# Routing the last quarter of the tokens of four mixtures of experts through sorted tiles

## The reference, cut to what matters

```
xn     = layernorm(x)
logits = xn @ gate_w + gate_b              # 16 experts (layers 0, 3) or 8 (layers 1, 2)
i0, i1 = the two largest logits            # gates g0, g1 = softmax over these two
layers 0, 3 (SwiGLU):  f_e(t) = (silu(t @ w1[e]) * (t @ w2[e])) @ w3[e]       # hidden 128
layers 1, 2 (GELU):    f_e(t) = gelu(t @ W1[e] + b1[e]) @ W2[e] + b2[e]       # hidden 256
x     += g0 * f_i0(xn) + g1 * f_i1(xn)
```

## Time and profile before

| | us |
|---|---|
| median of 3 runs | 1806.35 |
| lowest, highest | 1804.22, 1815.67 |
| span of the profiled execution | 1807.2 |
| TensorE matmuls busy | 1678.7 (93%) |
| VectorE busy | 1077.2 (60%) |
| ScalarE busy | 966.8 (53%) |
| GpSimd busy | 871.1 (48%) |

### The profile page before, as it was taken

How to read it: one execution, slowest core, us unless ns; L and a number is a source line. 1 busy time by engine, 2 the same in 40 slices (tenths; PEclk the granted TensorE clock), 3 DMA queues, 4 the chain that set the end, 5 groups by cost and what they waited for, 6 DMA issues and landing times. The chain is left out here.

```text
span 1807.2 us, 32921 instructions
## 1 busy us (share of the span) xinstructions
PE 1678.7 (93%) x12503; PEld 955.4 (53%) x12503; DVE 1077.2 (60%) x1532; ACT 966.8 (53%) x1427; POOL 871.1 (48%) x730
## 2 busy tenths in 40 slices
PE   5879999999689999998999997999999769999998
PEld 3635555554244444444444445777777535555554
DVE  6667777766863332365334236666656467777766
ACT  2545555555236666526666645666666355555554
POOL 3318887877025333313333335333323008877777
PEclk8999999999799999998999998999999879999999
DMA  5004343333202222401222340000000004333333
GB/s 126 1 15 118 108 111 111 110 109 101 74 1 79 90 83 66 103 2 32 93 79 67 96 95 1 1 2 1 2 1 1 3 5 122 116 118 116 114 116 103
DMA packets 74948, 121.64 MB, mean 67 GB/s; under 512 B 18306, under 2 KB 22594, under 8 KB 74146
## 3 DMA queue, kind: packets, MB, share of 16 engines
q1 hardware_dynamic: 74786, 119.48, 22.7%
HBM read 115.74 MB, written 3.67 MB: 66 GB/s over the span
## 5 line engine op out<-in xcount | busy, mean ns | idle before, releaser
L766 POOL TENSOR_TENSOR x<-x,mx_gated 128x512 f32<-128x512 f32 x254 | 326.7, 1286 | 85.6 <-DVE mx_gated L718 83.4
L711 DVE TENSOR_TENSOR mx_hidden<-ps,mx_hidden 128x1024 f32<-128x1024 f32 (+1 forms) x256 | 246.2, 962 | 177.2 <-PE ps L579 176.7
L579 PE MATMUL ps<-tokens_high,w_high 64*128 64x512 f32 x1536 | 330.9, 427 | 8.7 <-ACT mx_hidden L873 5.0
L873 ACT ACTIVATE mx_hidden<-ps,w_bias 128x1024 f32<-128x1024 f32 x256 | 264.1, 1115 | 124.8 <-PE ps L579 124.8
L579 PE MATMUL ps<-tokens_high,w_low 64*128 64x512 f32 x1536 | 305.7, 393 | 0.0
L579 PE MATMUL ps<-tokens_low,w_high 64*128 64x512 f32 x1536 | 305.5, 393 | 0.0
L919 POOL TENSOR_TENSOR x<-x,mx_gated 128x512 f32<-128x512 f32 x126 | 161.5, 1282 | 253.3 <-DVE mx_gated L891 253.3
L891 DVE SCALAR_TENSOR_TENSOR mx_gated<-ps,w_bias,mx_gates 128x512 f32<-128x512 f32 x128 | 96.0, 750 | 280.1 <-PE ps L843 260.6
L694 ACT ACTIVATE mx_hidden<-ps 128x1024 f32<-128x1024 f32 x256 | 248.5, 1022 | 15.4 <-PE ps L579 1.4
L1884 DVE TENSOR_TENSOR c_near_weights<-c_near_hats 128x768 f32<-128x768 f32 x192 | 190.0, 1037 | 102.8 <-PE ps L1755 102.8
L648 PE MATMUL ps<-mx_hidden,w_second 128*64 128x512 f32 x1024 | 248.4, 605 | 0.4 <-DVE mx_hidden L711 0.4
(11 more groups left out here) (225 smaller groups left out, 1905.6 us busy)
## 6 DMA issues: line engine op xcount, KB each, us to landing
mx_gates<-gate_board SPq DMA_DIRECT2D x768, 128.0 KB, 3.1
w_first<-in_f_first SPq DMA_DIRECT2D x4, 1024.0 KB, 11.6
c_weight<-in_c_weight SPq DMA_DIRECT2D x1, 2304.0 KB
x<-in_x SPq DMA_DIRECT2D x8, 256.0 KB, 5.8
w_second<-in_f_second SPq DMA_DIRECT2D x4, 512.0 KB, 13.3
w_first<-in_f_first SPq DMA_DIRECT2D x4, 512.0 KB, 9.8
out_x<-x SPq DMA_DIRECT2D x16, 128.0 KB, 2.7
gate_board<-xn SPq DMA_DIRECT2D x56, 16.0 KB, 2.1
```

Source lines behind the costliest of these rows:

```text
L579: last = pe.matmul(out[h], weights[w][half(h), w_own], tokens[t][half(h), t_own], start=(p == 0), stop=(p == 2))
L711: dve.tensor_tensor(own, second[:, 0:halves, :], own, ALU.mult).then_inc(s.hidden.semaphore, 1)
L766: pool.tensor_tensor(place, place, gated[:, n % GATED, :], ALU.add).then_inc(s.added.semaphore, 1)
L873: act.activation(hidden[:, n % HIDDEN, f], first[:, (n * F + f) % BLOCKS], ACT.Gelu, bias=w.bias1[:, e * F + f:e * F + f + 1]).then_inc(s. ...
```

## The change

Of each layer's 8 chunks, 6 stay dense. The tokens of the last two (2048 tokens, 4096 pairs of token and expert) are sorted by expert:

1. TensorE transposes the normed tokens (lay: 8 transposes) and ScalarE copies them.
2. The choice of the last pair of chunks is made first, and 24 small VectorE operations and two matmuls against a triangle of ones (op, count_up) give each pair its slot. Each expert starts a new tile of 256 slots, so there are 32 tiles in a SwiGLU layer (16 + 16 experts) and 24 in a GELU layer.
3. GpSimd writes the tokens to a DRAM board with 32 indirect DMAs of 128 rows of 256 bytes (scatter). SyncE loads the board back (load, 3 or 4 DMAs of 512 KB) and fetches each tile's expert weights through a register (fetch: two register reads and four DMAs for a turn, a ring of 6 turns).
4. All engines leave the dense loop at one point (step 60 of 96, or 30 of 48) for a phase of 16 (GELU: 12) turns of two tiles, in plain float32. For each turn TensorE makes 2 transposes, 4 matmuls of 256 columns, 2 (GELU: 4) output matmuls of 256 columns and 2 transposes back. ScalarE copies the columns, activates and copies the output. VectorE multiplies (SwiGLU) and copies the turned tile.
5. SyncE stores the result to a second board, GpSimd gathers it with 32 indirect DMAs, VectorE weighs it (2 operations per unit, 2 units), TensorE transposes and sums it (merge: 16 matmuls in all), and VectorE adds it to x (by.add).
6. While GpSimd issues indirect DMAs, VectorE makes the adds of the dense steps (by_vector): steps 30 to 53 and 60 to 83 of a SwiGLU layer, steps 15 to 25 and 31 to 41 of a GELU layer.
7. The sorted board is filled with zeros once, during conv0 (4 DMAs of 512 KB). The banks of PSUM 6 and 7 are handed out by a list (OutBanks), and semaphores of conv0 are used again.

```diff
+        self.dense = CHUNKS - 2 * sorted_pairs
+        self.sorted_tiles = sorted_pairs * 2 * HALVES * CHUNK // P
+        self.tiles = self.sorted_tiles + experts
+        self.slots = 2 * self.tiles
+SWIGLU = Mixture(experts=16, hidden=128, sorted_pairs=1)
+GELU = Mixture(experts=8, hidden=256, sorted_pairs=1)
...
+class ByExpert:
+    TILE = 2 * P
+    RING = 6
+    GROUP = 16
+    def scatter(self, pool, i):
+        choice, t = i % 2, i // 2
+        if i == 0:
+            pool.wait_ge(self.k.cleared, self.k.cleared_all)
+            self.s.rows.wait(pool, 1)
+            self.s.laid.wait(pool, self.UNITS)
+        pool.indirect_dma_start(out=self.sorted_board, in_=self.laid[:, t // HALVES, half(t % HALVES)], in_offset=None,
+                                out_offset=bass.IndirectOffsetOnAxis(ap=self.rows[:, choice, t:t + 1], axis=0)).then_inc(
+                                    self.s.scattered.semaphore, 16)
+    def gather(self, pool, i):
+        unit, choice, t = i // 16, i % 2, i // 2
+        if i == 0:
+            self.s.stored.wait(pool, 16 * (self.m.slots // self.GROUP))
...
+    def fetch(self, sp, u):
+        if u == 0:
+            self.s.expert.wait(sp, 1)
+        if u >= self.RING:
+            self.s.out.wait(sp, u - self.RING + 1)
+        for a in range(2):
+            tile = a * self.TURNS + u
+            e = sp.value_load(self.expert[0:1, tile:tile + 1], min_val=0, max_val=self.E - 1)
+            landed = self.s.weights[u % self.RING].semaphore
+            sp.dma_start(self.first[half(a), u % self.RING, :],
+                         self.first_of[bass.ds(e, 1)].rearrange("e c n -> (e c) n")).then_inc(landed, 16)
+            sp.dma_start(self.second[:, u % self.RING, a, :],
+                         self.second_of[bass.ds(e, 1)].rearrange("e c n -> (e c) n")).then_inc(landed, 16)
+    def load(self, sp):
+        self.s.scattered.wait(sp, 16 * 2 * self.NT)
+        for g in range(self.m.slots // self.GROUP):
+            sp.dma_start(self.own_group(g), self.group(self.sorted_board, g)).then_inc(self.s.loaded[g].semaphore, 16)
+    def phase_tensor(self, pe):
...
+        columns(0)
+        for u in range(TURNS):
+            if u + 1 < TURNS:
+                columns(u + 1)
+            first_layer(u)
+            if u >= 1:
+                second_layer(u - 1)
+            if u >= 2:
+                turn_back(u - 2)
...
...
+    TURN_AT, AFTER = 9, 60
+    LAY_AT, COUNT_AT, MERGE_AT = (4, 6), 19, (77, 87)
+    SCATTER_AT, GATHER_AT, EACH = 32, AFTER + 2, 3
+    by = ByExpert(k, ctx, m, name, layer, top_two, hidden[:].rearrange("p r h c -> p (r h c)"), fetch_at=(38, 40, 42, 44, 46, 48), load_at=54, after=AFTER)
+    def by_vector(n):
+        return SCATTER_AT - 2 <= n < SCATTER_AT + ROUNDS or GATHER_AT - 2 <= n < GATHER_AT + ROUNDS or n == STEPS - 1
...
+        def gate_both(n):
+            gate(n)
+            gate(n + 1)
+            for a in (n, n + 1):
+                if by_vector(a):
+                    gates.add(dve, a, gated[:, a % GATED, :])
...
+            for a in (n - 3, n - 2):
+                if a >= 0 and not by_vector(a):
+                    gates.add(pool, a, gated[:, a % GATED, :])
+            for i in range(EACH):
+                if 0 <= (n - SCATTER_AT) // 2 * EACH + i < MOVES:
+                    by.scatter(pool, (n - SCATTER_AT) // 2 * EACH + i)
+                if 0 <= (n - GATHER_AT) // 2 * EACH + i < MOVES:
+                    by.gather(pool, (n - GATHER_AT) // 2 * EACH + i)
...
+    TURN_AT, AFTER = 3, 30
+    LAY_AT, COUNT_AT, MERGE_AT = (4, 6), 9, (39, 44)
+    SCATTER_AT, GATHER_AT, EACH = 15, AFTER + 1, 3
+    by = ByExpert(k, ctx, m, name, layer, top_two, hidden[:].rearrange("p r f h c -> p (r f h c)"), fetch_at=(16, 18, 20, 22, 23, 24), load_at=26, after=AFTER)
```

More of the change, by code:

```diff
@@ new lines, with __init__, bank, free @@
+class OutBanks:
+    def __init__(self, k, order, by_expert):
+        self.k, self.order, self.by_expert = k, order, by_expert
+        self.at = {use: i for i, use in enumerate(order)}
+    def bank(self, *use):
+        return self.k.ps[:, 6 + self.at[use] % 2, :]
+    def free(self, pe, *use):
+        i = self.at[use] - 2
+        if i < 0:
+            return
+        what, n = self.order[i]
+        if what == "step":
+            self.k.mx.gated.wait(pe, n + 1)
+        elif what == "gates":
+            self.k.mx.rows.wait(pe, n + 1)
+        elif what == "lay":
+            self.k.by.laid.wait(pe, n + 1)
+        elif what == "count":
+            self.k.by.counted.wait(pe, n + 1)
+        elif what == "phase":
+            self.k.by.turned.wait(pe, self.by_expert.TURNS)
+        elif what == "merge":
+            self.k.mx.merged.wait(pe, n + 1)
@@ L581, in split_product, with out_order, mixture_swiglu @@
     return last
-def mixture_swiglu(k, ctx, w, tokens, top_two, following):
+def out_order(steps, E, dense, turn_at, lay_at, count_at, after, merge_at):
+    order = [("gates", 0)]
+    for n in range(steps):
+        order.append(("step", n))
+        if n % E == turn_at and n // E + 1 < dense:
+            order.append(("gates", n // E + 1))
+        if n in lay_at:
+            order.append(("lay", lay_at.index(n)))
+        if n == count_at:
+            order += [("count", 0), ("count", 1)]
+        if n == after - 1:
+            order += [("phase", 0), ("phase", 1)]
+        if n in merge_at:
+            order.append(("merge", merge_at.index(n)))
+    return order
+def mixture_swiglu(k, ctx, w, layer, tokens, top_two, following):
     nc, x, s = k.nc, k.x, k.mx
-    E = SWIGLU.experts
+    m = SWIGLU
+    E, DENSE = m.experts, m.dense
     FIRST, HIDDEN, OUT, GATED, KEPT = 2, 4, 2, 3, 2
-    STEPS = CHUNKS * E
+    STEPS = DENSE * E
     name = f"mx{k.mixtures}_"
@@ L842, in second_layer @@
                 for h in range(HALVES):
-                    last = pe.matmul(out[half(h), slot(n), :], w.second[:, (e * F + f) * C:(e * F + f + 1) * C],
+                    last = pe.matmul(out.bank("step", n)[half(h), :], w.second[:, (e * F + f) * C:(e * F + f + 1) * C],
                                      hidden[:, n % HIDDEN, f, h, :], start=(f == 0), stop=(f == F - 1))
             last.then_inc(s.third.semaphore, 1)
-            if e == TURN_AT and i + 1 < CHUNKS:
-                s.gated.wait(pe, n)
-                gates.turn(pe, i + 1, out[:, turn_slot(i + 1), :])
+            if e == TURN_AT and i + 1 < DENSE:
+                out.free(pe, "gates", i + 1)
+                gates.turn(pe, i + 1, out.bank("gates", i + 1))
+            if n in LAY_AT:
+                unit = LAY_AT.index(n)
+                out.free(pe, "lay", unit)
+                by.lay(pe, unit, out.bank("lay", unit))
+            if n == COUNT_AT:
+                for c in range(2):
+                    out.free(pe, "count", c)
+                    by.count_up(pe, c, out.bank("count", c))
+            if n in MERGE_AT:
+                unit = MERGE_AT.index(n)
+                out.free(pe, "merge", unit)
+                by.merge(pe, unit, out.bank("merge", unit))
         for n in range(0, STEPS, 2):
```

793 lines of the change are left out of this document (616 added, 177 removed).

## The result

The changed kernel takes 1904.48 us (median of 4 runs, 1901.09 to 1910.55), against 1808.03 us (4 runs) before: a ratio of 1.054, 95% interval 1.051 to 1.057. It is slower by 96 us, where 1778 us was predicted, with a range to 1838. The profiled execution has a span of 1908.8 us.

What follows compares the result with a forecast made beforehand. TensorE, busy 93% of the span, was taken as the bound. Removed dense chunks against added work gave -8.7 us a SwiGLU and -6.6 a GELU layer, twice each, plus 1.5 at the end: 1778 us, range 1735 to 1838.

Steps and rivals of the forecast that it cites:

- A round with VectorE's adds: SwiGLU dense loop: two adds between gates and multiply lengthen a round from 4.86 to 5.56 us, 16.8 us a layer.
- the 0.28 us of lead: SwiGLU round: VectorE's second add would start at 1795.27, before GpSimd's multiply at 1795.55, so VectorE is first.
- most groups fit, and for the longer ones ... I add 4 us: SwiGLU dense loop: sort and choice operations fit VectorE's 1.41 us wait between multiplies; longer groups add 4 us.
- the rival of the adds: SwiGLU rounds: VectorE's second add waits up to 1.3 us for GpSimd's multiply; total 1840 us, chance 0.12.
- a fetch is then 2.7 us: SyncE, expert weights: four DMAs at 0.43 us and two register reads at 0.5 each, more than a SwiGLU turn.
- 3.4 us late: SwiGLU phase: last weights land at 36.4 us where TensorE wants them at 33.0; 3.4 us added to the phase.
- This rival: Late weights: register reads of 1.5 us make a fetch 4.7; SwiGLU phase grows 20 us; total 1830, chance 0.12.
- just hidden: GELU layer: three indirect DMAs at 1.1 us fill a 3.3 us step; 32 scatters end after 35 of 37 us.
- the adds are free: GELU layer: VectorE needs 0.75 + 0.69 of 3.3 us, so its adds fit; 1 us taken.
- From about 1.35 us on the gain is gone: GpSimd's scatters and gathers: the forecast gain vanishes if indirect DMAs take about 1.35 us or more each.
- the highest: Rival on GpSimd's scatters and gathers: indirect DMAs take 1.7 us each; total 1884 us, chance 0.14.
- slow indirect DMAs: At 1.7 us each, GELU scatters take 54 us not 37, gathers 59 not 40: 33 us a layer; chance 0.14.

Runs made afterwards that it cites:

- the experiment: Changed kernel with GpSimd's adds and its half of the product in a SwiGLU layer's first 30 steps replaced by fills (GELU adds too, first 15): 1880.86 us.
- the last experiment: Changed kernel with VectorE's adds made after the odd step's multiply, SwiGLU fetches spread out and the GELU load three steps later; result kept whole: 1877.75 us.
- the fixed experts: Changed kernel with each tile's weights fetched from an expert given by tile number, without a register read, so wrong weights are used: 1864.50 us.
- short adds: Changed kernel with VectorE's adds of dense steps covering 8 of 512 columns: 1865.23 us.

## Why the prediction was wrong

**The terms that held.** A round with VectorE's adds takes 5.62 us (5.56 predicted); without them a SwiGLU layer loses 14.5 us (16.8), and less because GpSimd is next at 5.1. The chain of waits of the changed kernel runs there through the two adds into the multiply and on to TensorE's products, as the prediction has it. A turn of TensorE takes 2.23 us (2.1). A GELU phase takes 37.5 and 38.0 us from the last dense product's end to the next dense product (38.6). The adds mostly didn't wait for GpSimd where the change put them (median 0.69 us), as the 0.28 us of lead said. GpSimd's multiply waited for them instead, 1.60 us against 1.29. The adds' own wait comes when they are moved.

**The step that failed most: "most groups fit, and for the longer ones ... I add 4 us".** The front of a SwiGLU layer grew by 22.2 us, of which 2.4 were counted for lay and count and 4 for this. The number of operations was no fault: three of them at 0.42 us fit a round of 4.86 us. Their price was. They were sized as if they stood alone, at 0.42 us; beside GpSimd's readers they take 1.15 to 1.27, which costs at least 12.5 us a layer. The row that said so was in hand: 174 ns at best and 1150 in the median. I used it for the rival of the adds, not for the two dozen small operations that have the same two inputs. Of the other 9.5 us, about 5 stand in the rounds of lay and count, whose term of 2.4 was about half of what they took, and the rest in rounds whose operations the experiment still held up. The Trainium skill ("SBUF — State Buffer", Who interferes with whom) has the rule, that a VectorE instruction with two SBUF inputs and a GpSimd one that reads SBUF exclude each other; these traces agree (0.425 against 1.2 us).

**SyncE: "a fetch is then 2.7 us".** It is 3.8: a read costs 0.74 and not 0.5, and a DMA of the fetch 0.57 and not 0.43. "3.4 us late" became some 12.8 us of first layers (45.9 against 33.1), and the phase 53.3 us, from the last dense third product at 1742.32 to the next dense product at 1795.62, and not 44.3. This rival was priced about right: at 4.7 us a fetch I had given it 20 us of phase, which makes 11 at 3.8, and it came to 9. What the sum had not at all is that fetches ahead of time, made in the scatter's rounds, push the gates back: the scatter stretch is 66.7 us, while the gather's, with as many DMAs and no fetch, is 59.3. The 7.4 us between them went when the order was changed.

**GELU: "just hidden" and "the adds are free".** Thirty-two scatters at 1.27 us take 41 us, not 35, and the load stands at 37. "From about 1.35 us on the gain is gone" had the point too high, since the queue behind the load, with gates needed four steps later, was left out of it. Moving the load gives 9.4 to 13.4 us a layer back, and 9.6 and 9.7 in the last experiment. The adds cost 5.4 us and not 1; 2 to 2.4 of the 5.4 are in the stretches of the scatters and gathers, and why a layer that has slack on VectorE loses the rest is not settled.

**The sum.** For a SwiGLU layer, 15.8 (front beyond 6.4) + 1.4 (24 rounds at 5.62 instead of 5.56) + 7.4 + 9.0 (phase) = 34 of the 38 to 40 us between the forecast and the measured layer. For a GELU layer, 9.4 to 13.4 for the load and 4.4 for the adds are 14 to 18 of 24 to 25; with the fixed experts another 3 to 6 us went, which may overlap with the load's and is little more than these layers vary by. The rest, 4 to 7 us of a SwiGLU and 7 to 10 us of a GELU layer, is in the merge and around the phase and has no experiment of its own. The lower clock, 0.90 to 0.92 where TensorE had waited, is part of these stretches' times and was in no term of the sum. No single rival reached 1904 us either: the highest stood at 1884. What came was several of them in part, beside the small operations' price, which none of them had. Two slips of the working change nothing here: 16 x 2.1 is 33.6 and not 33.4, and 17 and 19 us of slow indirect DMAs are 36 a GELU layer and not 33.

## What to carry to other kernels

Before small operations are put into an engine's gaps, take their price from the slowest rows of their kind beside the other engine's work, and fill the gaps round by round, not on average: here a gap of 1.41 us took three operations at their single price, or one at its blocked price. When a queue carries both far-ahead and just-in-time transfers, count what each new entry, and each wait in it, delays of the others. A change that takes work from the bounding engine and spreads additions over all others must be summed against every engine's slack in each stretch: here VectorE, busy for 57.5 of 78.8 us of the front before, became the bound.

## What the runs showed of the hardware

- A VectorE operation of 128x256 with two SBUF inputs takes 0.425 us beside GpSimd's fills, which read nothing, and 1.15 to 1.27 in the mean between GpSimd's tensor operations. An operation that follows another one waits again.
- GpSimd's fills go with another block: a VectorE TENSOR_SCALAR of 128x16 took 2.36 us and one of 128x32 2.2 us, through GpSimd's multiply and the fill behind it, where the first took 1.18 with an add behind the multiply, and 0.17 was its least. The section named above has VectorE's 2-port mode contend with GpSimd, which these rows fit; no run shows the mode that these operations ran in.
- GpSimd pays as well: its multiply of 128x512 takes 1.29 us in the median beside short adds, 1.60 behind VectorE's whole adds in the changed kernel, and 1.77 where the adds were moved onto it.
- An indirect DMA of 128 rows occupies GpSimd for 0.96 us, and 1.27 us pass from one to the next. The Trainium skill ("DMA: Bandwidth & Descriptors", Latency and other measured facts) has about 1 us for the first byte of GpSimd's own DMA emission; the 0.96 us of the row is how long GpSimd is held and not when the first byte moves, but it comes out near that, and the 0.30 us between two of them come on top.
- A register read, with the addresses made from it, adds 0.74 us on SyncE to two DMAs. With fixed addresses the same DMAs are issued every 0.57 us, where the opening loads stand 0.48 apart.
